# An attention block on one core: two operand buffers at other addresses, one copy earlier in the second group's queue, and ScalarE's heads ahead of the late exponentials

## The reference

```python
def _L0_cond_ref(x, attn_bias, mask, g_in, null_attn_bias, null_kv, Wq, Wkv, Wo, g_out):
    xn = layernorm(x, g_in)                       # x: 64 batches of 128 tokens, 512 wide
    q = (xn @ Wq).reshape(b, n, H, DH).transpose(0, 2, 1, 3) * scale   # H = 16 heads of DH = 64
    k, v = split(xn @ Wkv)                        # one key and value head for all 16
    k, v = concat([null_k, k]), concat([null_v, v])
    sim = einsum('bhid,bjd->bhij', q, k) + concat([null_bias, attn_bias])
    sim = where(causal_mask | key_mask, -max, sim)
    out = einsum('bhij,bjd->bhid', softmax(sim), v)
    return layernorm(out.transpose(0, 2, 1, 3).reshape(b, n, INNER) @ Wo, g_out)
x = x + _L0_cond_ref(...)
```

## Time and profile before

| | us |
|---|---|
| median of 3 runs | 1016.31 (1016.21 to 1018.83) |
| the profiled execution's own time | 1017.48 |
| its span, first to last instruction | 1015.7 |
| TensorE busy | 989.0 (97% of the span) |
| GpSimd busy | 834.8 (82%) |
| VectorE busy | 767.9 (76%) |
| ScalarE busy | 658.6 (65%) |
| mean granted TensorE clock | 0.995 of full |

### The profile page before, as it was taken

The page is one execution under the profiler, slowest core; times in us unless marked ns, Lnnn a source line. Parts: engine busy times, 40 slices in busy tenths (PEclk is TensorE's granted clock), DMA queues, the critical chain, the costliest instruction groups (busy, mean ns, idle before and its releaser), DMA issues.

```text
span 1015.7 us, 43757 instructions
## 1 busy us (share of the span) xinstructions
PE 989.0 (97%) x14250; PEld 869.1 (86%) x14250; DVE 767.9 (76%) x3553; ACT 658.6 (65%) x2622; POOL 834.8 (82%) x1503
## 2 busy tenths in 40 slices
PE   7889999999999999999999999999999999999987
PEld 5879888888888888888888888888888888888875
DVE  5976787777887777787777887777787777786664
ACT  5846676665676665676665676666676666675563
POOL 4877888888888888888888888888888888888786
PEclk9998999999999999999999999999999999999999
DMA  8422223223232332323323232232323223222112
GB/s 240 118 79 73 86 72 87 82 68 98 64 107 73 80 87 60 105 69 87 79 70 96 68 106 72 76 90 55 109 70 86 78 71 96 68 70 67 37 44 63
DMA packets 93774, 84.04 MB, mean 83 GB/s; under 512 B 25328, under 2 KB 67824, under 8 KB 93552
## 3 DMA queue, kind: packets, MB, share of 16 engines
q1 hardware_dynamic: 92496, 81.05, 29.9%
q10 hardware_dynamic: 1056, 0.04, 0.1%
HBM read 40.12 MB, written 16.78 MB: 56 GB/s over the span
## 4 chain that ended last, share of the span: by engine, by line
PE 89%; POOL 4%; SPq 3%; issue 2%; DVE 1%; DMA 1%; ACT 1%; POOLq 0%; DVEq 0%; ACTq 0%
PE ps_proj L569 39%; PE ps_pv L546 22%; PE ps_pv L553 11%; PE ps_s L507 10%; PE ps_pv L532 8%; SPq L369 1%; POOL bias_b L1222 1%; POOL w_nrm L1231 1%; DMA q_sb<-in_fside_16xSxS_dram 0%; SPq L344 0%; SPq L379 0%; SPq L338 0%; POOL bias_c L1320 0%; POOL y_nrm L1271 0%; POOL y_out L1275 0%
## 5 line engine op out<-in xcount | busy, mean ns | idle before, releaser
L1031 ACT ACTIVATE exp_bot<-logit_bot,neg_max 128x129 f32<-128x129 f32 x512 | 201.4, 398 | 211.0 <-DVE neg_max L693 208.2
L1222 POOL TENSOR_TENSOR bias_b<-bias_c,mask_add 128x256 f32<-128x256 f32 (+1 forms) x512 | 297.9, 612 | 26.8 <-DVE neg_max L693 26.4
L569 PE MATMUL ps_proj<-xt_hi,wq_hi 128*128 128x256 f32 x1024 | 299.0, 292 | 6.0 <-ACT v_raw L1083 3.7
L569 PE MATMUL ps_proj<-xt_hi,wq_lo 128*128 128x256 f32 x1024 | 285.0, 278 | 0.0
L569 PE MATMUL ps_proj<-xt_lo,wq_hi 128*128 128x256 f32 x1024 | 284.6, 278 | 0.0
L693 DVE CUSTOM_DVE_ANT_0 logit_bot<-ps_s,bias_b 128x128 f32<-128x128 f32 x512 | 128.5, 289 | 139.7 <-PE ps_s L507 123.1
L569 PEld LDWEIGHTS ps_proj<-xt_hi,wq_hi 128*128 128x128 f32 x1024 | 193.4, 189 | 21.2 <-issue 10.5
L1231 POOL TENSOR_TENSOR w_nrm<-exp_bot,w_inv 128x256 f32<-128x256 f32 x256 | 157.9, 617 | 63.0 <-DVE w_inv L702 61.6
L546 PE MATMUL ps_pv<-wo_hi,o_hi 128*128 128x512 f32 x488 | 194.1, 398 | 1.5 <-DVE o_lo L715 1.4
L569 PEld LDWEIGHTS ps_proj<-xt_hi,wq_lo 128*128 128x128 f32 x1024 | 194.0, 189 | 0.7 <-issue 0.5
L569 PEld LDWEIGHTS ps_proj<-xt_lo,wq_hi 128*128 128x128 f32 x1024 | 193.6, 189 | 0.0
(11 more groups left out here) (114 smaller groups left out, 1747.3 us busy)
## 6 DMA issues: line engine op xcount, KB each, us to landing
x_in<-in_x_dram SPq DMA_DIRECT2D x32, 512.0 KB, 4.1
x_split<-xn SPq DMA_DIRECT2D x480, 32.0 KB, 1.9
v_rep<-v_raw SPq DMA_DIRECT2D x256, 32.0 KB, 1.9
x_res<-in_x_dram SPq DMA_DIRECT2D x128, 64.0 KB, 1.9
x_res<-in_x_dram SPq DMA_DIRECT2D x64, 128.0 KB, 2.6
out_dram<-y_out SPq DMA_DIRECT2D x128, 64.0 KB, 1.7
out_dram<-y_out SPq DMA_DIRECT2D x64, 128.0 KB, 2.3
w_raw<-in_L_cond_Wq_dram SPq DMA_DIRECT2D x4, 512.0 KB, 7.6
```

The source lines that it names most:

```text
L569: mm = pe.matmul(ps[:, 0:TOK], w[:, k, cols], xt[:, slot, k], start=(j == 0), stop=(j == len(todo) - 1))
L1031: ins = nc.scalar.activation(out_[:, s, j], in_[:, s, j], ACT.Exp, bias=neg_max[:, s, k:k + 1], scale=-1.0, accum_out=w_sum[:, s, k:k + 1])
L1222: ins = nc.gpsimd.tensor_tensor(out_, bias, key_mask, ALU.add)
```

## The change

It has four parts. (1) On ScalarE, at the steps `t % 8 == 6`, `heads_hi` goes ahead of the late exponentials, as it already does at `t % 8 == 2`. These are the only two steps of a group that have heads. There are 30 steps of this kind in the lists and the loop: `t` = 14 of pair 0, `t` = 6 and 14 of the pairs 1 to 14, and `t` = 6 of pair 15. (2) On SyncE's queue, in the second group, `spread_v(1)` goes ahead of the mask load, of the 16 transfers of `split_x(3)` and of an x load. (3) GpSimd's difference `wo_lo` in the first group waits until VectorE has made the other three. (4) Three unused strips: 64 bytes ahead of `q_sb`, 32 ahead of `wt`, and 64 instead of 32 ahead of `o_hi`. By the built program `q_sb` and `wt` then start on a multiple of 128 bytes, `keys` and `v32` stay at 64 past one, and `o_hi` is again at 64 past one. The small buffers between `q_sb` and `wt` move by 64 bytes, those behind `wt` by 128.

```diff
+        apart_from_keys = sb("apart_from_keys", [P, 16])
         q_sb = sb("q_sb", [P, 2, CB, 2, TOK])
...
+        apart_from_v = sb("apart_from_v", [P, 8])
         wt = sb("wt", [P, 2, WBLOCKS, CB, BLK])
-        apart_from_wo = sb("apart_from_wo", [P, 8])
+        apart_from_wo = sb("apart_from_wo", [P, 16])
...
                 if first:
                     split_x(BY_PE)
                     next_x(0)
+                    spread_v(2 * p + 1)
                     next_mask()
                     split_x(2 * p + 3)
                     next_x(1)
-                    spread_v(2 * p + 1)
...
                 for t in steps(first, last):
                     n = CP * p + t
-                    if t < CP and t % CG != STEP_HEADS:
-                        exponentials(n, t, 1)
                     for batch, back in due("heads", p, t, first, last):
                         for g in range(4):
                             heads_hi(batch, g)
-                    if t < CP and t % CG == STEP_HEADS:
+                    if t < CP:
                         exponentials(n, t, 1)
-                    if t < CP:
                         exponentials(n, t, 0)
...
                 pool.wait_ge(wo_hi_made, WP)
+                pool.wait_ge(wo_lo_made, WP - 1)
                 nc.gpsimd.tensor_tensor(wo_piece(wo_lo, WP - 1), raw_piece(WP - 1, OT // WP),
```

## The result

The changed kernel took 1011.92 us (median of 6 runs, 1010.17 to 1014.71), the kernel before on the same chip 1017.31 us (median of 6, 1015.83 to 1018.83). The ratio is 0.9949 with a 95% interval of 0.9929 to 0.9968. So it is faster, by 5.4 us and not by the 11.9 forecast. The profiled execution took 1014.71 us for a span of 1012.9.

A forecast was written before the change was run, and what follows sets the result against it. TensorE, busy 989.0 of 1015.7 us, was taken as the bound. Terms -5.1 - 6.5 - 0.3 + 0 = -11.9 us gave 1004.4 us against a median of 1016.31, with an 8-in-10 range of 998 to 1010.

The forecast's parts named there:

- Part 1: Heads ahead of late exponentials: first eight project_out matmuls after t % 8 == 6 fall to 1.83 us, 30 pieces, -5.1 us.
- the `inverse` of step 7 will wait some 0.4 us: On VectorE, inverse waits for the later exponentials, some 0.4 us a group, at no cost to TensorE.
- Part 2: Earlier spread_v(1) in the second group: no v_raw wait, scores blocks 6.49 instead of 13.03 us apart, -6.5 us.
- 5.25 us of holes: SyncE's queue, second group: the copies' 5.00 us fit idle stretches of 5.25, so x_split still starts at about 56.0.
- called its pause short: Second group: VectorE's list up to step 12's logits delays TensorE's banks by a short pause at most; ends -4.5 to -7.5.
- 13.03 us: Second group: distance between two scores blocks, 70.92 to 83.95, read as the whole loss including the reduced clock.
- the second group's gain is passed on: Rival, 10%: x_split slips 5 us or VectorE becomes the next wait; some 1.5 of 6.5 us remain, 1009.4 us.
- The mask load's slip: SyncE's queue, second group: the mask load behind the copies moves from 53.98 to some 55.6, given as about 1.9 us.
- Part 3: GpSimd's wait for wo_lo, first group: up to 1.4 us won, mostly given back waiting for x_split; -0.3 us.
- Part 4: Operand distances of scores and values: nothing in the rows tells distance from no distance; 0 us, ends -11 and +3.
- upper end of +3: Scores matmuls: 0.03 ns more for each of 768 columns, 128 blocks, +3 us.

The follow-up runs named there:

- e6: Kernel before with only spread_v(1), the eight v_rep copies, moved ahead of the mask load, x_split and an x load: 1011.09 us, ratio 0.997.
- e4: Kernel before with only o_hi and o_lo moved 128 bytes further: 1017.08 us, ratio 1.0021.
- e5: Kernel before with only the heads put ahead of the late exponentials at t % 8 == 6: 1009.59 us, ratio 0.9944.
- e12: e11 with o_hi and o_lo moved 128 bytes too, so they lie 192 bytes from wo_hi modulo 256: ratio to before 0.9899.
- e11: Changed kernel, second group's copies and x_split ahead of its loads, o_hi/o_lo and wo_hi/wo_lo each 128 bytes further (distance 64 modulo 256): ratio to before 0.9953.
- e2: Kernel before with only the three unused strips added, lists as before: 1017.07 us, ratio 1.0027.
- e1: Changed kernel's lists with the buffers at the addresses of the kernel before: 1006.9 us, ratio 0.9915.
- e9: Changed kernel, second group's copies and x_split ahead of its loads, o_hi at wo_hi's place modulo 256 (distance 0): 1002.38 us, ratio to before 0.9883.
- e15: e9 with xt_hi and xt_lo moved 128 bytes, to 64 bytes behind the projection weights modulo 256: 1008.64 us, ratio to before 0.9921.
- e7: Kernel before with only GpSimd's wait for VectorE's wo_lo added: 1014.72 us, ratio 1.0002.

## Why the prediction was wrong, by its own steps

The direction, faster, was right; the time of 1004.4 us was not, and 1011.92 lies outside 998 to 1010. Two steps failed, for about 3.5 us each.

- *Part 1, -5.1 us: right.* Measured alone -5.7. The mechanism held at each point: 1.64 us from `values` to `o_hi`, VectorE free in time. That "the `inverse` of step 7 will wait some 0.4 us" came out at 0.58, and TensorE did not feel it. What I had not seen is the `xt_lo` behind it, which now runs beside GpSimd and takes 32 us more in all; that too stayed off TensorE's path.
- *Part 2, -6.5 us: more than twice what came.* Measured alone -3.0. The step that failed is "5.25 us of holes, and the copies take 5.00 ... and the sixteen `x_split` start at about 56.0 as before". I took the 5.00 us from one row and filled the holes to within 0.25 us. The same trace has the same eight copies at 5.42 to 6.05 us in 29 of its 32 groups. At their new place they took 5.83 to 7.00 us, and `x_split` started at 57.42 (e6) and 57.92 (after). Nothing was left to take that up, in front of a transfer for which VectorE waited already. Behind `x_turned` stand the statistics, `v` and the `logits` of step 12, and then the copies of `q_sb` that free TensorE's banks. I had named that list and called its pause short; it was 1.52 us, and with it the distance of the scores blocks stayed at 8.29 us and not 6.49. That is 1.8 us of the error. The other 1.6 us are the measure: 13.03 us was the longest of five executions with that queue, whose median is 11.45. The rival "the second group's gain is passed on", to which I gave 10%, has the right mechanism, VectorE as the next wait and a pause further on, but not the right size: it left 1.5 us of gain, for a slip of 5 us, and the slip was 1.3 to 1.8. (The mask load's slip, from 53.98 to 55.6, is 1.6 us and not the 1.9 that I wrote; nothing hangs on it.)
- *Part 3, -0.3 us: not contradicted.* Alone it measured 0.0, with an interval of 0.1% each way, and 0.3 us is too small to be seen in it. The pause of 1.41 us that I read in one trace is missing in two others without the wait (e4, e5), and where it stands it lies ahead of the wait for `x_split`. How much each of the two has in the result is not shown.
- *Part 4, 0 us: right for the matmuls it looked at, wrong as a term.* Scores and `values` did not change. The step that failed is "**Term: 0**" for all addresses together. Three pads moved everything behind them, and I asked only about the two tile pairs that the change names, not what stands last in the row. `o_hi` and `o_lo` went 128 bytes on. I had counted places modulo 128, by which they stood where they were, and the pace of `project_out` tells 128 bytes apart. Its 24 matmuls a block are more of the chain than scores and `values` together. The cost is 0.09 us a block, 5.5 us by count. Measured it was +5.5 us between e12 and e11, +2.7 in e2, and +3.5 us from e1 to the changed kernel (0.9915 and 0.9949, each against its own runs of the kernel before, give or take 3 us). My upper end of +3 was for another cause. I leaned on a rule of the Trainium skill (TensorE: Matmul & The Clock Gate, on what happens when you issue a matmul) by which weight loads take nothing from a running matmul. If neither read took anything from the other, the distance between the two operands should not count, and in e11 and e12 it did: the same instructions with the same weight loads took 5.36 and 5.27 us a block. So these runs speak against resting a term of zero on that rule for 128x128 tiles of fp32r. Whether it is the weight load that takes the time, they do not show.

The sum by measured parts: -5.7 - 3.0 + 0.0 + 3.5 = -5.2 us; measured were -5.2 us by the ratio and -5.4 by the medians. Since the 3.5 is itself the changed kernel less e1, what this tests is the lists: -8.7 us in parts and -8.6 together.

## What to carry to other kernels

An unused tile moves everything behind it: before timing one, list every tile whose place changes and every matmul that reads it, and put a second pad behind the pair so that the rest stays. To fill a queue's hole with a transfer, read the transfer's time in all groups of the trace and not in one row (here 4.96 to 6.05 us), and ask what the thing behind it costs per us of lateness; a hole that fits to within 5% does not fit. A stretch at a reduced clock differs in length between executions, so a distance in one profile is not the gain: of the four executions of e9 two had a mean clock of 0.999 and took 1000.9 and 1001.6 us, and two had 0.996 and took 1003.2 and 1003.8.

## What the runs showed of the hardware that was not expected

Where two SBUF operands of a 128x128 fp32r matmul begin, modulo 256 bytes, changes the pace at which such matmuls follow each other, without any wait in the profile: by up to 2.5% for 512 columns (5.23 to 5.36 us for 23 distances) and 5% for 256 columns (5.65 to 5.95 us for 48). The order of the four distances differs between the two forms. Counted as streamed operand beyond the weights, it is 0, 64, 128, 192 bytes from fast to slow in `project_out` (in the table above, weights beyond the streamed operand, these are 0, 192, 128, 64), and 192 and 64 fast, 128 and 0 slow in the projections. Scores and `values`, fp32 in tiles of 64 and 32 rows, showed nothing. Why the orders differ was not tried; the weights' slices and the time of a load within the stream differ between the forms, and the runs do not separate them. The eight copies of 32 KB between partitions took 4.96 to 6.05 us to issue in the 32 groups of before, and 5.62 to 7.00 us at their early place in the second group; a single issue among them can last 2.25 us (after) or 1.77 (e6) where the others last 0.6. A VectorE and a GpSimd difference that start within 0.01 us of each other take 3.46 and 2.38 us or 1.22 and 3.46 us.

The length of a pause of TensorE alone did not tell whether the granted clock falls. In the second group, from 68 to 82 us, it stayed at 1.00, the level of 2.4 GHz, with longest pauses of 1.52 (e6), 2.56 (e1) and 2.93 us (e2). It had a mean of 0.88 with 1.88 (e9) and 1.95 us (e15), and also with 2.82 (after), 3.17 (e7) and 3.48 us (e5). It had 0.76 with 3.63 (e4) and 3.67 us (before).
